# The softmax sums' reciprocals take another way to the columns of the output: by transfers through DRAM instead of TensorE, ScalarE and GpSimd

## The reference

```python
x = x + 0.5 * ffn(layernorm(x))
q, k, v = heads(x_n @ wq.T), heads(x_n @ wk.T), heads(x_n @ wv.T)      # 16 heads of 64
q, k = rotary(q), rotary(k)
scores = where(causal, (q @ k.T) / 8, -inf)
out = (softmax(scores) @ v) @ wo.T
x = x + out
x = x + 0.5 * ffn(layernorm(x))
```

## Time and profile before

| | us |
|---|---|
| median of three runs | 1323.15 (1322.53 to 1323.75) |
| the profiled execution | 1324.65 |
| its span, first to last instruction | 1322.9 |
| attention's steady loop body, two pairs | 67.9 |
| PE busy, of the span | 1247.7 (94%) |
| ACT, DVE, POOL busy | 914.8, 754.2, 444.5 |

### The profile page before, as it was taken

The page is one execution under the profiler, slowest core; times in us unless marked ns, Lnnn a source line. Parts: engine busy times, 40 slices in busy tenths (PEclk is TensorE's granted clock), DMA queues, the critical chain, the costliest instruction groups (busy, mean ns, idle before and its releaser), DMA issues. The chain is left out here.

```text
span 1322.9 us, 26897 instructions
## 1 busy us (share of the span) xinstructions
PE 1247.7 (94%) x7456; PEld 869.4 (66%) x7456; DVE 754.2 (57%) x1787; ACT 914.8 (69%) x1946; POOL 444.5 (34%) x288
## 2 busy tenths in 40 slices
PE   5986699999999999999999999999999999999898
PEld 2543566777777677767676767676767676766465
DVE  5574446665556666565656565656565656554354
ACT  3654467777777777777777777777777777777574
POOL 5132443333333333333333333333333333330000
PEclk8997799999999999999999999999999999999999
DMA  7122444454544445454545454545454544431000
GB/s 275 45 95 88 124 104 130 110 134 107 142 106 129 121 110 140 97 146 104 145 105 145 105 145 105 145 105 145 105 144 104 135 107 130 108 84 36 1 29 36
DMA packets 107198, 147.80 MB, mean 112 GB/s; under 512 B 11808, under 2 KB 61344, under 8 KB 107040
## 3 DMA queue, kind: packets, MB, share of 16 engines
q1 hardware_dynamic: 106768, 146.65, 41.8%
q10 hardware_dynamic: 400, 0.79, 0.3%
HBM read 36.24 MB, written 10.49 MB: 35 GB/s over the span
## 5 line engine op out<-in xcount | busy, mean ns | idle before, releaser
L936 DVE CUSTOM_DVE_ANT_0 probs<-wide,tri_mask 128x1024 f32<-128x1024 f32 (+7 forms) x512 | 386.0, 756 | 431.3 <-PE wide L637 424.8
L821 ACT ACTIVATE probs<-probs,neg_max 128x1024 f32<-128x1024 f32 (+7 forms) x512 | 395.6, 774 | 160.8 <-DVE neg_max L936 156.8
L832 ACT ACTIVATE shared_a<-bank 128x512 f32<-128x512 f32 (+2 forms) x640 | 339.6, 548 | 111.6 <-PE bank L653 107.8
L653 PE MATMUL bank<-ident,probs 128*128 128x128 f32 x2304 | 366.0, 278 | 3.5 <-ACT shared_a L832 1.3
L653 PEld LDWEIGHTS bank<-ident,probs 128*128 128x128 f32 x2304 | 266.2, 141 | 153.3 <-issue 108.6
L636 PE MATMUL wide<-k_hh,q_hl 128*128 128x512 f32 (+3 forms) x768 | 292.6, 383 | 5.9 <-DMA k_hh<-parts 2.2
L670 PE MATMUL bank<-shared_a,v_cur 128*64 128x256 f32 (+3 forms) x1792 | 297.2, 453 | 0.0
L637 PE MATMUL wide<-k_low,q_hl 128*128 128x512 f32 (+3 forms) x768 | 257.9, 343 | 0.0
L92 POOL TENSOR_TENSOR rotated<-terms,cross 128x1024 f32<-128x1024 f32 x62 | 147.7, 2383 | 291.0 <-DVE cross L86 282.8
L670 PEld LDWEIGHTS bank<-shared_a,v_cur 128*64 128x64 f32 x1792 | 108.7, 136 | 113.2 <-issue 88.2
L1049 POOL COPY inv_wide<-inv 128x512 f32<-128x512 f32 x64 | 39.1, 611 | 376.0 <-DVE inv L944 343.4
(11 more groups left out here) (114 smaller groups left out, 1323.6 us busy)
## 6 DMA issues: line engine op xcount, KB each, us to landing
q_hl<-parts SPq DMA_DIRECT2D x254, 128.0 KB, 2.8
k_hh<-parts SPq DMA_DIRECT2D x254, 128.0 KB, 2.7
v_cur<-shared_b SPq DMA_DIRECT2D x32, 512.0 KB, 5.8
k_low<-parts SPq DMA_DIRECT2D x63, 256.0 KB, 4.2
xn_cur<-xn_scratch SPq DMA_DIRECT2D x15, 1024.0 KB, 5.8
w_qk<-w_scratch SPq DMA_DIRECT2D x32, 256.0 KB, 3.1
w_scratch<-first_w_parts SPq DMA_DIRECT2D x8, 512.0 KB, 3.1
xn_scratch<-shared_a SPq DMA_DIRECT2D x8, 512.0 KB, 3.1
```

Of the source, the lines that this page charges most:

```text
L653: last = nc.tensor.transpose(ring[at % 2][:, col:col + P], probs[g][:, h, OFFSET[g][r] + j * P:OFFSET[g][r] + (j + 1) * P], ident[:])
L821: nc.scalar.activation(own, own, ACT.Exp, bias=neg_max[g][:, col], scale=-1.0, accum_out=sums[g][:, col]).then_inc(probs_done, 1)
L832: nc.scalar.activation(turned[:, slot, to], ring[at % 2][:, 0:w * len(heads)], ACT.Copy).then_inc(ring_free[at % 2], signals)
L936: nc.vector.tensor_tensor_reduce(out=part_of_probs(g, k), in0=wide_banks[k % 2][:, x0:x1], in1=tri_mask[:, SEQ - (x1 - x0):], scale=1.0, s ...
```

## The change

POOL's spread, PE's transposes and ACT's copy are gone. In their place SP sends `inv` to a small DRAM tensor in transposed order (`send_inv`, one DMA of 128 x 8 elements of 4 bytes) and, when that has landed, reads it back (`spread_inv`), each row of 128 values repeated over the 64 partitions of a head, by one DMA for each head. `inv_sum` is double, one for each group. `normalise` waits for the two reads instead of ACT's copy. The ring loses two places, so the turns of group 1 move by one place to the other bank. On the queue, group 0's send stands between the copies of chunk 0 and of chunk 1, its reads between chunk 1 and `k_low`; group 1's send and reads stand at the end of the pair, behind the weights and `xn_cur` and ahead of the next pair's copies.

```diff
-        RING = [[0, 1, 2, 3, 4, 5, 6, 8, 9, 10], [12, 13, 14, 15, 16, 17, 18, 19, 20, 22]]
-        RING_SUM, RING_OUT = [11, 23], [21, 7]
-        NR = 24
+        RING = [[0, 1, 2, 3, 4, 5, 6, 8, 9, 10], [11, 12, 13, 14, 15, 16, 17, 18, 19, 21]]
+        RING_OUT = [20, 7]
+        NR = 22
...
-        inv_wide = sb("inv_wide", [P, 8, HEAD_DIM])
-        inv_sum, head_out = sb("inv_sum", [P, CHUNK]), sb("head_out", [P, CHUNK])
+        inv_sum = [sb(f"inv_sum{g}", [P, CHUNK]) for g in range(2)]
+        head_out = sb("head_out", [P, CHUNK])
...
-            def turn_sums(p, g):
-                at = RING_SUM[g]
-                pe.wait_ge(inv_spread, 2 * p + g + 1)
-                may_write(p, at)
-                for r in range(4):
-                    last = nc.tensor.transpose(ring[at % 2][:, P * r:P * (r + 1)],
-                                               inv_wide[:, 2 * r:2 * r + 2, :].rearrange("p h d -> p (h d)"), ident[:])
-                last.then_inc(ring_full, 1)
...
             def invert(p, g):
                 dve.wait_ge(probs_done, unit(p, g, 7))
-                if some(2 * p + g):
-                    dve.wait_ge(inv_spread, 2 * p + g)
+                if some(p):
+                    dve.wait_ge(inv_sent[g], 16 * p)
                 nc.vector.reciprocal(inv[g][:], sums[g][:]).then_inc(inv_done, 1)
 
             def normalise(p, g):
-                dve.wait_ge(ring_free[1], bank_count(p, RING_SUM[g]))
+                dve.wait_ge(inv_back[g], 32 * p + 32)
                 dve.wait_ge(out_step, NK * p + KEYS[0] + KEYS[1] * g)
-                nc.vector.tensor_tensor(head_out[:], out_bank[:], inv_sum[:], ALU.mult).then_inc(head_done, 1)
+                nc.vector.tensor_tensor(head_out[:], out_bank[:], inv_sum[g][:], ALU.mult).then_inc(head_done, 1)
...
+            def send_inv(p, g):
+                sp.wait_ge(inv_done, 2 * p + g + 1)
+                if some(p):
+                    settle(sp)
+                    sp.wait_ge(inv_back[g], 32 * p)
+                sp.dma_start(inv_dram[g].rearrange("r q -> q r"), inv[g][:],
+                             allow_slow_non_contiguous=True).then_inc(inv_sent[g], 16)
+
+            def spread_inv(p, g):
+                sp.wait_ge(inv_sent[g], 16 * p + 16)
+                if some(p):
+                    settle(sp)
+                    sp.wait_ge(head_done, 2 * p + g - 1)
+                for h in range(2):
+                    sp.dma_start(inv_sum[g][HEAD_DIM * h:HEAD_DIM * (h + 1), :].rearrange("d (r q) -> d r q", r=4),
+                                 inv_dram[g].rearrange("(r h) q -> h r q", h=2)[h:h + 1].to_broadcast([HEAD_DIM, 4, P])
+                                 ).then_inc(inv_back[g], 16)
+
...
-                if has_next and not (first and u == 0):
+                fills = has_next and not (first and u == 0)
+                if fills:
                     may_fill(p + 1)
-                    for c in range(2):
-                        for h in range(2):
-                            fill_qk(sp, o, 1 - u, c, h)
+                    for h in range(2):
+                        fill_qk(sp, o, 1 - u, 0, h)
+                send_inv(p, 0)
+                if fills:
+                    for h in range(2):
+                        fill_qk(sp, o, 1 - u, 1, h)
+                spread_inv(p, 0)
+                if fills:
                     for h in range(2):
                         fill_low(sp, o, 1 - u, h)
...
+                send_inv(p, 1)
+                spread_inv(p, 1)
```

More of the change, by code:

```diff
@@ L507, in _, with attention @@
                         sp.wait_ge(stored[u], 16 * PAIRS_OF_CHUNKS)
-def attention(nc, x, xn_dram, xn_stored, wo_pairs, ahead_of, o, constants,
+def attention(nc, x, xn_dram, xn_stored, inv_dram, wo_pairs, ahead_of, o, constants,
               turned_mem, v_stage, wide_banks, banks):
@@ L557, in attention @@
         ring_full, ring_free = sem("ring_full"), [sem(f"ring_free{b}") for b in range(2)]
-        out_step, inv_done, inv_spread, head_done = sem("out_step"), sem("inv_done"), sem("inv_spread"), sem("head_done")
+        out_step, inv_done, head_done = sem("out_step"), sem("inv_done"), sem("head_done")
+        inv_sent, inv_back = ([sem(f"{n}{g}") for g in range(2)] for n in ("inv_sent", "inv_back"))
         AHEAD_UNITS = [(0, n) for n in range(6)] + [(None, 0), (None, 1), (1, 0), (1, 1), (None, 2), (None, 3)] + [
@@ L737, in pair @@
                 ahead(3)
-                turn_sums(p, 0)
                 times_v(p, i, u, 0, 2)
@@ L767, in pair @@
                 next_score(6)
-                turn_sums(p, 1)
                 next_score(7)
@@ L833, in keep_turned @@
                                      ACT.Copy).then_inc(ring_free[at % 2], signals)
-            def keep_sums(p, g):
-                at = RING_SUM[g]
-                act.wait_ge(ring_full, ring_count(p, at))
-                if some(2 * p + g):
-                    act.wait_ge(head_done, 2 * p + g)
-                nc.scalar.activation(inv_sum[:], ring[at % 2][:], ACT.Copy).then_inc(ring_free[at % 2], 1)
             def pair(i, u, first, last):
@@ L875, in pair @@
                 exponential(p, 1, 7)
-                keep_sums(p, 0)
                 keep_turned(p, u, 1, 0)
@@ L899, in pair @@
                 next_exponential(6)
-                keep_sums(p, 1)
                 ahead_v(3)
@@ L1040, in rope_half, with pair @@
                 low_half(nc, o, c)
[L1042 to L1058, removed]
+            def pair(i, u):
+                for c in range(2):
+                    rope_half(i + 1, u, c)
             pool.wait_ge(high_done, 2)
@@ L1068, in _ @@
             for u in range(2):
-                pair(0, u, False)
+                pair(0, u)
             with pool.Fori(1, ALL_PAIRS // 2 - 1) as i:
                 for u in range(2):
-                    pair(i, u, False)
-            for u in range(2):
-                pair(ALL_PAIRS // 2 - 1, u, True)
+                    pair(i, u)
         @block.sync
@@ L1157, in macaron @@
     xn_dram = nc.dram_tensor("xn_scratch", [P, 2, TOKENS], F32, kind="Internal").ap()
+    inv_dram = [nc.dram_tensor(f"inv_scratch{g}", [8, P], F32, kind="Internal").ap() for g in range(2)]
     w_split = nc.dram_tensor("w_scratch", [PAIRS, P, 2, 512], F32, kind="Internal").ap()
@@ L1253, in macaron @@
         first_half.close()
-        attention(nc, x, xn_dram, xn_stored, wo_pairs, ahead, o,
+        attention(nc, x, xn_dram, xn_stored, inv_dram, wo_pairs, ahead, o,
                   (tri_mask, ident), shared_a, v_stage, wide_banks, banks[4:8])
```

## The result

The changed kernel takes 1683.11 us (median of four runs, 1676.97 to 1687.48) against 1322.84 (also four runs): a ratio of 1.272, 95% interval 1.268 to 1.277. The forecast was 1340 with a range of 1300 to 1395, so the direction was right and the size far off, beyond the range.

A forecast was written before the change was run, and what follows sets the result against it. PE bounds the kernel now; after the change the SP queue would, making two pairs 69.2 us against 67.88: +18.6 us over 14 odd pairs, -4 us elsewhere, in all +15, so 1340 us, range 1300 to 1395.

The forecast's parts named there:

- What bounds the kernel, and the gain on PE: Attention loop: PE, busy 67.0 of 67.9 us, sets the time; removing its transposes saves it 2.77 us per two pairs.
- rival 3: SP queue has more spare time than reckoned, so PE stays the bound: 1280 us; chance 0.04.
- The queue as the place: SP queue sets the interval: sends and waits delay the next pair's copies, +1.33 us per two pairs; chance 0.64.
- the forecast's sum: Intervals between pairs' first scores: even 34.7 us, odd 34.5 us, together 69.2 against 67.88; whole kernel +15 us.
- Rival 2: Second send's pieces overtake the 1 MB xn_cur load on the SP queue: even interval 31.7 us, kernel 1295 us; chance 0.10.
- The pieces: A send's 1024 pieces of 4 bytes take 1.2 us on the DMA engines, bounds nothing and 1.72 us.
- The sign that I had named for this case: In the changed kernel's timeline, sends landing more than 5 us after their turn would show dear small pieces.
- Rival 1: Small pieces of a send are dear: 1385 us at twice a 512-byte piece, about 1560 at four times; chance 0.22.
- DVE's wait, costed at nothing: DVE's normalise of group 1 waits for the spreads; they come about a microsecond ahead, so no cost.
- Rival 4: Pieces at nothing and a 4.6 us landing bring two pairs to about 67.9 us, within 0.2%; that outcome had 0.08.

## Why the prediction was wrong

**What bounds the kernel, and the gain on PE: right.** With the queue out of the way two pairs take 65.3 and 65.6 us, where the forecast had 65.11 for PE without its transposes (31.03 + 34.08), and the kernel takes 1284 to 1285 us, where rival 3 had 1280.

**The queue as the place: right.** PE waits just ahead of a pair's first scores, for `k_low`; SP waits for the landing of the sends; the copies stand behind. With cheap pieces the forecast's sum is near: 1350 measured, 1340 forecast. There the intervals are 34.3 and 35.5 us on average against 34.7 and 34.5, and what the odd one has more is the clock's. Rival 2, the pieces that overtake the load, falls: in that kernel the reads start 5.4 us after their send behind `xn_cur`, and 2.5 us after it without.

**The pieces: the step that failed.** I set the 1024 pieces of 4 bytes at 1.2 us, between nothing and 1.72 us, the 512-byte piece at full bandwidth. The measured price, at the second send of an even pair with only weights ahead, is 10.26 us from issue to the reads (748.29 to 758.55), where rows of 32 bytes have 2.51 at the same place (678.29 to 680.80): about 8 us more. That is over four times the upper bound, and it comes at both sends of a pair, at the first of them half covered by chunk 1. The mistake wasn't only the size. I bounded the price by what pieces take on the DMA engines, and there nothing contradicts the bound: the engines are done 2.7 us after the issue, as with spaced pieces. The time that I had no term for lies between that and the landing, 7.6 us in which the engines are idle. Bandwidth rows of transfers that write whole rows say nothing about when the last of a thousand small neighbouring writes is reported as done. The sign that I had named for this case, sends that land more than 5 us after their turn, is what the trace shows.

Rival 1 named this, "dear pieces", and gave 1560 us at four times the 512-byte piece; with the clock kept up the kernel takes 1574 us. That the two are so near is partly luck, since the rival priced time on the engines and the trace shows time after them. It had 0.22, and the range ended at little over twice that piece. The Trainium skill's rule that I cited there (DMA: Bandwidth & Descriptors, Specifications) makes every transfer under 512 bytes a read-modify-write. No run shows whether that happens, and the rule alone doesn't part the runs, since all their pieces are under 512 bytes: 4-byte pieces 16 bytes or more apart land within 4 us, and only those 4 bytes apart take some 10. The Trainium skill's other rule that I cited (the same page, Rules for kernel authors, one descriptor per element) agrees with the trace, whose page counts 80416 packets under 512 bytes where the kernel before had 11808. It doesn't part the runs either: all the spaced ones have 1024 pieces as well.

**The clock: a term that the sum didn't have.** I priced PE's waits at their own length, and took PE's work at the price of the earlier trace rows, where the clock is 1.00. With the wait of 7.1 us the clock was granted at 0.50 in the stretch of the wait and 0.55 in the 5 us that follow, and PE's work is 71.8 us per two pairs, where it is 65.2 and 65.4 at a clock of 1.00 in the two versions without these waits. Filling the wait with useless products gave 109 us back. The same term is in the kernel with rows of 32 bytes, in which moving one send won 66 us instead of the 25 to 42 that I expected.

**DVE's wait, costed at nothing: wrong with slow sends** (5.39 us at 718.13, PE behind it), by way of the same term.

**Three details of the rivals don't hold**, and nothing hangs on them here. Rival 4's pieces at nothing and landing of 4.6 us give 33.1 + 34.1 = 67.2 us, not 67.9. Rival 1's half microsecond for the first group's spreads is 0.2 (3.1 + 3.4 less 1.14 + 5.18). And against rival 2 I said that no later DMA of this queue ends ahead of an earlier one; the trace of the kernel before has one that does, near its start: `w_v`, issued at 158.91, lands after 5.0 us, and the first `q_hl` behind it, issued at 159.56, after 3.3.

What remains open is which neighbours collide, and where the writes stand in the seven idle microseconds.

## What to carry to other kernels

When a step leaves the busiest engine for a DMA queue, look first at what stands behind it on that queue: one small send behind a 1 MB load, and a wait for it ahead of the next copies, cost 66 us in the kernel with rows of 32 bytes, and moving it ahead of that load turned a loss of 2% into a gain of 3%. (That kernel has its values at the wrong columns; the version with rows of 128 bytes has the same time with the right ones.) A transfer whose pieces are single words next to each other in DRAM is to be avoided even at 4 KB; turn the words on an engine that has time to spare (0.21 us on DVE) and send rows. Idle DMA engines don't mean that a transfer has landed: look at when what waits for it begins. And a stall of TensorE can be dearer than its length, as those of 2 to 7 us were here in most pairs: look at the granted clock in the stretch behind it.

## What the runs showed of the hardware that was not expected

- Reads that wait for 1024 writes of 4 bytes side by side in DRAM start 10.26 us after the send, and the DMA engines show no work for the last 7.6 of them; 16, 32, 64 and 512 bytes apart a send lands in 3.9, 3.3, 3.2 and 3.2 us, 8 bytes apart in SBUF in 2.5 us, and as 128 rows of 32 bytes in 2.1 us.
- While such a send is under way, copies behind it on the queue show as busy engines (0.94) that move 39 GB/s, and `k_low` lands in 8.8 us instead of 4.2 even where nobody waits for the send.
- TensorE's granted clock was 0.50 in a stretch in which PE was busy for 0.90 of 5 us, and 0.55 in the next 5 us of full work; over two whole pairs it was 0.87, and 0.98 where useless products filled most of the wait. Behind two waits of 2.20 and 2.28 us in one run it was 0.95 and 1.00 over the interval that follows.
